# Turned blocks of experts, x and y in pieces of 512 bytes: contraction tiles that hold every fourth unit

## The reference

```
x = x + (x @ W[cat] + b[cat])                       # layer 0: W[cat] is 512 x 512
h = gelu(x @ fc1_w.T + fc1_b)                       # 512 -> 2048, exact gelu
x = x + concat(h @ fc2_w.T + fc2_b,                 # 2048 -> 384, shared
               h @ experts_w[e].T + experts_b[e])   # 2048 -> 128, the batch's expert (128 x 2048)
```

## Time and profile before

| | |
|---|---|
| median of three runs | 1680.95 us |
| profiled execution | 1681.4 us |
| its span, first to last instruction | 1679.6 us |
| granted TensorE clock, mean | 0.997 |
| DMA packets, bytes | 884,826, 243.44 MB |

### The profile page before, as it was taken

One profiled execution on the slowest core, in us unless ns is written; L12 is line 12 of the kernel. 1 busy time (PEld: TensorE's weight loads), 2 busy tenths in 40 slices (PEclk: granted clock), 3 DMA queues, 4 the chain that ended last, 5 costly groups with the idle time before them and its releaser, 6 DMA issues.

```text
span 1679.6 us, 28015 instructions
## 1 busy us (share of the span) xinstructions
PE 1639.4 (98%) x7065; PEld 1315.8 (78%) x7065; DVE 1176.4 (70%) x2004; ACT 551.9 (33%) x927; POOL 195.1 (12%) x195
## 2 busy tenths in 40 slices
PE   7899999999999999999999999999999999999999
PEld 5778887877878778787877878778787787878887
DVE  5677667776777767776776677767777677767754
ACT  4343333333323333333332333333333333333321
POOL 0200100111020010200102001110200102001110
PEclk9999999999999999999999999999999999999999
DMA  7886776757677575775767767686775757757630
GB/s 207 185 190 150 147 149 147 156 129 162 127 163 151 131 156 118 167 159 133 149 133 160 156 144 157 131 157 135 163 153 131 155 118 164 163 131 151 134 61 26
DMA packets 884826, 243.44 MB, mean 145 GB/s; under 512 B 803688, under 2 KB 818168, under 8 KB 884732
## 3 DMA queue, kind: packets, MB, share of 16 engines
q1 hardware_dynamic: 740732, 203.75, 57.1%
q10 hardware_dynamic: 144000, 38.82, 10.7%
HBM read 209.93 MB, written 32.51 MB: 144 GB/s over the span
## 4 chain that ended last, share of the span: by engine, by line
PE 66%; SPq 20%; issue 8%; DMA 3%; DVE 2%; ACT 1%; DVEq 0%
PE ps_out L814 30%; PE ps_h L799 14%; PE ps_e L799 13%; PE ps_y L786 8%; SPq L386 8%; SPq L341 4%; SPq L320 2%; DMA e_blocks<-in_L_cond_experts_w 2%; SPq L399 2%; SPq L351 1%; SPq L393 1%; PE ps_t L745 1%; DVE e_whole L643 1%; DVE h L599 1%; DVE w2e L599 1%
## 5 line engine op out<-in xcount | busy, mean ns | idle before, releaser
L814 PE MATMUL ps_out<-w2e,h 128*128 128x512 f32 x3072 | 758.0, 396 | 10.0 <-DVE h L599 10.0
L814 PEld LDWEIGHTS ps_out<-w2e,h 128*128 128x128 f32 x3072 | 574.3, 188 | 152.5 <-DVE h L599 15.9
L799 PE MATMUL ps_e<-y_t,w 128*128 128x512 f32 x1536 | 376.8, 395 | 1.4 <-DVE y_t L599 1.4
L799 PE MATMUL ps_h<-y_t,w 128*128 128x512 f32 x1536 | 375.7, 394 | 0.0
L799 PEld LDWEIGHTS ps_e<-y_t,w 128*128 128x128 f32 x1536 | 290.7, 189 | 66.9 <-DVE y_t L599 1.6
L799 PEld LDWEIGHTS ps_h<-y_t,w 128*128 128x128 f32 x1536 | 288.5, 188 | 65.7
L643 DVE STREAM_TRANSPOSE e_whole<-e_blocks 128x512 f32<-128x512 f32 x256 | 182.0, 711 | 109.3 <-DMA e_blocks<-in_L_cond_experts_w 100.9
L530 ACT CAST w2e<-e_whole 128x512 fp32r<-128x512 f32 x256 | 158.6, 620 | 284.4 <-PE ps_out L814 157.4
L463 POOL TENSOR_TENSOR x_raw<-x_raw,b_all 128x512 f32<-128x512 f32 x60 | 85.3, 1422 | 1354.9 <-DMA x_raw<-in_x 1303.2
L499 ACT CAST w_split<-w_raw 128x512 fp32r<-128x512 f32 x244 | 145.7, 619 | 243.7 <-DMA w_raw<-in_L_cond_W 174.4
L599 DVE TENSOR_TENSOR w_split<-w_raw,w_split 128x512 fp32r<-128x512 f32 x244 | 161.1, 688 | 84.6 <-ACT w_split L499 83.7
(11 more groups left out here) (71 smaller groups left out, 431.3 us busy)
## 6 DMA issues: line engine op xcount, KB each, us to landing
e_blocks<-in_L_cond_experts_w SPq DMA_DIRECT2D x1024, 64.0 KB, 2.9
w_raw<-in_L_cond_W SPq DMA_DIRECT2D x248, 256.0 KB, 2.9
out<-resid SPq DMA_DIRECT2D x64, 256.0 KB, 4.7
x_blocks<-in_x SPq DMA_DIRECT2D x240, 64.0 KB, 2.4
b_all<-in_L_cond_b SPq DMA_DIRECT2D x60, 256.0 KB, 4.3
x_raw<-in_x SPq DMA_DIRECT2D x60, 256.0 KB, 4.6
y_rows<-y ACTq DMA_DIRECT2D x60, 256.0 KB, 2.8
x_blocks<-y_rows ACTq DMA_DIRECT2D x240, 64.0 KB, 3.7
```

The source lines that it names most:

```text
L799: last = nc.tensor.matmul(h_bank(c)[:, :], w1[:, w, k, c * P:(c + 1) * P], y_t[:, a, k, :, :].rearrange("p b s -> p (b s)"), start=(k == 0 ...
L814: last = nc.tensor.matmul(ps_out[b][:, :], h[:, c % 2, a, b * S:(b + 1) * S], fc2_columns(c, c % 2, w, b), start=(c == 0 and n == 0), stop ...
```

## The change

Contraction tile k now holds the units 4p + k, for partition p. The same holds for the hidden units: tile c of quad u holds the units 512u + 4p + c % 4. The sum over units is the same, in another order. A quad of an expert is then 512 hidden units in a row, and a block's piece in the loads is 128 elements, 512 bytes, of which DVE's transpose takes every fourth. TensorE's transposes read every fourth column of the tile. Rows of layer 0's weights and of fc1_w come four apart, fc2_w in rows of 2 KB; fc1_b goes directly to b1, in pieces of four values.

```diff
-        b1_rows = x_raw[0:NC, 0:P]
...
-        def hidden_rows(c):
-
-            return (c % QUAD) * (NC // QUAD) + c // QUAD
+        def every_fourth(whole, k):
+
+            return whole.rearrange("p (m k) -> p k m", k=KD)[:, k]
 
         def prep_src(t):
             if PREP[t][0] == "fc1":
-                m = hidden_rows(PREP[t][1])
-                return fc1_w[m * P:(m + 1) * P, :]
+                m = PREP[t][1]
+                return fc1_w.rearrange("(u p c) d -> u c p d", u=NC // QUAD, c=QUAD)[m // QUAD, m % QUAD]
             _, n, q = PREP[t]
-            return fc2_w[n * P:(n + 1) * P, :].rearrange("p (k u h) -> u p k h", k=QUAD, h=P)[q]
+            return fc2_w[n * P:(n + 1) * P, q * QUAD * P:(q + 1) * QUAD * P]
...
-                    src = x[bass.ds(G * GB + b, 1), :, :].rearrange("o (j q) (k i r) -> i q k (o j) r", q=Q, k=KD, r=Q)[i]
-                    sp.dma_start(x_blocks[i * Q:(i + 1) * Q, :].rearrange("q (k j r) -> q k j r", k=KD, r=Q), src)\
+                    src = x[bass.ds(G * GB + b, 1), :, :].rearrange("o (j q) (i n) -> i q (o j) n", q=Q, n=P)[i]
+                    sp.dma_start(x_blocks[i * Q:(i + 1) * Q, :].rearrange("q (j n) -> q j n", n=P), src)\
...
-                sp.dma_start(w_slot(G, j), l0_w[bass.ds(cat, 1), k * P:(k + 1) * P, :].rearrange("o d n -> (o d) n"))\
+                src = l0_w[bass.ds(cat, 1), :, :].rearrange("o (p k) n -> k (o p) n", k=KD)[k]
+                sp.dma_start(w_slot(G, j), src)\
...
-                            .rearrange("o (j q) (c u i r) -> u i q c (o j) r", q=Q, c=QUAD, i=P // Q, r=Q)[quad, i]
-                        sp.dma_start(e_blocks[i * Q:(i + 1) * Q, quad % 2, b, :]
-                                     .rearrange("q (c j r) -> q c j r", c=QUAD, r=Q), src).then_inc(e_in[quad % 2], 16)
+                            .rearrange("o (j q) (u i n) -> u i q (o j) n", q=Q, i=P // Q, n=P)[quad, i]
+                        sp.dma_start(e_blocks[i * Q:(i + 1) * Q, quad % 2, b, :].rearrange("q (j n) -> q j n", n=P), src)\
+                          .then_inc(e_in[quad % 2], 16)
...
-                    sp.dma_start(b1_rows, fc1_b.rearrange("(c p) -> c p", p=P)).then_inc(b1_in, 16)
+                    sp.dma_start(b1[:, :].rearrange("p (u c) -> p u c", c=QUAD), fc1_b.rearrange("(u p c) -> p u c", p=P, c=QUAD))\
+                      .then_inc(b1_in, 16)
...
-                    src = y_rows[b, :, :].rearrange("(j q) (k i r) -> i q k j r", q=Q, k=KD, r=Q)[i]
-                    act.dma_start(x_blocks[i * Q:(i + 1) * Q, :].rearrange("q (k j r) -> q k j r", k=KD, r=Q), src)\
+                    src = y_rows[b, :, :].rearrange("(j q) (i n) -> i q j n", q=Q, n=P)[i]
+                    act.dma_start(x_blocks[i * Q:(i + 1) * Q, :].rearrange("q (j n) -> q j n", n=P), src)\
...
-                if j == 2:
-                    act.wait_ge(b1_turned, 1)
-                    nc.scalar.copy(b1[:, :], ps_e[:, 0:NC]).then_inc(b1_ready, 1)
             y_high(0, GB - 1)
-            act.wait_ge(b1_ready, 1)
+            act.wait_ge(b1_in, 16)
...
+            def split_of(whole_t):
+
+                return whole_t.rearrange("p (k j q) -> p k j q", k=KD, q=Q)
+
+            def blocks_of(blocks):
+
+                return blocks.rearrange("p (j r k) -> p k j r", k=KD, r=Q)
...
-                nc.vector.transpose(x_whole_t[:, :], x_blocks[:, :]).then_inc(x_turned, 1)
+                nc.vector.transpose(split_of(x_whole_t[:, :]), blocks_of(x_blocks[:, :])).then_inc(x_turned, 1)
...
-                nc.vector.transpose(dst, x_blocks[:, :]).then_inc(y_turned, 1)
+                nc.vector.transpose(split_of(dst), blocks_of(x_blocks[:, :])).then_inc(y_turned, 1)
...
-                off = (c % QUAD) * P
-                nc.vector.transpose(e_whole[:, :], e_blocks[:, (c // QUAD) % 2, :, off:off + P]).then_inc(e_turned, 1)
+                src = e_blocks[:, (c // QUAD) % 2, :, :].rearrange("p b (j r c) -> p c (b j) r", c=QUAD, r=Q)[:, c % QUAD]
+                nc.vector.transpose(e_whole[:, :].rearrange("p (a q) -> p a q", q=Q), src).then_inc(e_turned, 1)
...
-                turn(ps_t, [resid[:, b, k * P:(k + 1) * P] for k in range(KD)]).then_inc(x_turned, 1)
+                turn(ps_t, [every_fourth(resid[:, b, :], k) for k in range(KD)]).then_inc(x_turned, 1)
...
-                turn(y_bank(b), [y[:, b, k * P:(k + 1) * P] for k in range(KD)])\
+                turn(y_bank(b), [every_fourth(y[:, b, :], k) for k in range(KD)])\
...
-                turn(prep_bank(t), [prep_tile(t)[:, n * P:(n + 1) * P] for n in range(4)]).then_inc(prep_turned, 1)
+                turn(prep_bank(t), [every_fourth(prep_tile(t), k) for k in range(KD)]).then_inc(prep_turned, 1)
...
-                if j == 2:
-                    pe.wait_ge(b1_in, 16)
-                    nc.tensor.transpose(ps_e[:, 0:NC], b1_rows, ident[0:NC, 0:NC]).then_inc(b1_turned, 1)
```

More of the change, by code:

```diff
@@ L312, in load_prep @@
             after(eng, prep_turned, max(prep_earlier(t), default=-1) + 1)
[L313 to L314 removed]
+            eng.dma_start(prep_tile(t), prep_src(t)).then_inc(prep_in[prep_slot(t)], 16)
         @block.sync
```

8 lines of the change are left out of this document (1 added, 7 removed).

## The result

The changed kernel takes 1670.62 us (median of five runs, 1668.82 to 1672.98), the kernel before 1681.01 beside it: ratio 0.9937, 95% interval 0.9922 to 0.9952. That is 10.4 us faster, where 24 were forecast. The profiled execution took 1670.62 us, its span 1668.8.

A forecast was written before the change was run, and what follows sets the result against it. TensorE, 98% busy, was taken as the bound, losing time to waits behind DVE. 17.5 us in the loop's groups + 5.5 + 1.4 in group 0 = 24.4 us off 1681.4: 1657.0 us, range 1647 to 1679.

The forecast's parts named there:

- group 0: First group: a 3.40 us wait and 2.1 us of low clock go (5.5 us), plus a 1.4 us prepared-tile wait.
- the first stall: Step 3 of a group: fc2 waits for h_low behind DVE's late expert blocks; 0.65 us a group, to go.
- The floor: TensorE's time for a group without waits: 36 calls of 2.80 us, 100.8 us against 102.07, so 1.27 us lost.
- The second stall: Start of a group: TensorE waits for x_low behind layer 0's late-issued slices; 0.62 us a group, to go.
- the cover: SP's issue ahead of layer 0's slices: 24 DMAs save 0.25 us each, 6.0 us where 0.9 is needed.
- nothing added: DVE's transposes at a step of four stay at 711 ns; the other end was 0.53 us more each.
- covered: Weight rows 8 KB apart land nothing to 1 us later, hidden by SP coming 5 to 6 us earlier.
- 2d - 0.45: Stall in us at a group's start if each DVE transpose takes d longer; 1.7 where 0.62 stood for the third cycle.
- the other end: Upper bound for TensorE's own strided transposes: twice as long, 36 x 0.43 = 15.5 us; the forecast added nothing.
- The second cycle: Rival, chance 0.31: DVE's strided transposes take 0.53 us more each, only the first stall goes; 1669.6 us.
- The third cycle: Rival, chance 0.11: DVE's strided transposes take 1.07 us more each, the kernel gets slower; 1699 us.
- the unchanged issue time: Rival, chance 0.12: a block DMA holds SP as long as before, the stalls mostly stay; 1675 us.

The follow-up runs named there:

- experiment 3: The changed kernel with DVE's transposes reading runs and layer 0's slices loaded as 128 consecutive rows (units mixed, wrong result): 1656.43 us, ratio 0.9837.
- experiment 18: The changed kernel with layer 0 as before the change, and the experts' bias loads and batch 0's x load issued later: 1657.32 us, ratio 0.9857.
- experiment 1: The changed kernel with only DVE's transposes of experts, x and y reading runs again (units mixed, wrong result): 1664.34 us, ratio 0.9883.
- experiment 2: The changed kernel with only layer 0's slices loaded as 128 consecutive rows again (units mixed, wrong result): 1666.75 us, ratio 0.9903.
- experiment 17: The changed kernel with the experts' bias loads and batch 0's x load issued later: 1664.34 us, ratio 0.9898.
- experiment 15: The changed kernel with the experts' bias loads moved behind the next group's first slices and stores: 1666.80 us, ratio 0.9909.
- experiment 16: The changed kernel with layer 0 as before the change and the experts' bias loads moved behind the next group's first slices and stores: 1670.70 us, ratio 0.9930.
- experiment 5: The kernel before the change, unaltered, profiled once more to see what differs between executions: 1684.21 us.
- experiment 13: The changed kernel with each expert block DMA in 256 evenly spaced pieces of 256 bytes, pattern kept at three dimensions (wrong result): 1688.77 us, ratio 1.0035.
- experiment 14: The changed kernel with each experts' bias load cut into two loads of 128 pieces of 256 bytes: 1704.67 us, against 1687.61 for the kernel before.
- experiment 10: A change of the same kind with tiles of every second unit, pieces of 256 bytes and slice rows 4 KB apart: 1677.35 us, ratio 0.9954.

## Why the prediction was wrong

The forecast counts 17.5 us in the groups of the loop and 6.9 in group 0. Measured in the profiles, from the first call of layer 0 in one group to that of the group thirteen later, 11.1 us are won (167.27 to 1493.72 us before, 168.62 to 1483.99 after), 1.1 behind it, and 1.4 are lost ahead of it.

*What bounds the kernel, and the first stall: right.* TensorE's waits behind DVE were the loss, 19.6 us by their rows. The wait for h_low went whole, 10.0 us where 9.1 were counted, and with it DVE's wait for blocks. Block DMAs take SP 317 ns for 333 forecast, packets are 303,178 for 307,000, the DMA share from 128 to 1600 us fell from 0.69 to 0.52, for 0.47 forecast. The chain's call of fc2 doesn't come every 100.8 us yet: TensorE's calls behind x_low's wait stand at 269.80 and, eleven groups later, at 1383.27: (1383.27 - 269.80) / 11 = 101.2.

*The floor: 0.7 us a group too high.* "36 x 2.80 = 100.8" takes the longest calls for all. Without a wait a group takes 100.11 us in experiment 3 and 100.19 in experiment 18: calls of fc1 take 2.74 to 2.80 us, and one of layer 0 takes 1.38. So the kernel before lost 102.03 - 100.11 = 1.92 us a group, not 1.27, and the waits were worth more than was counted. This is why experiment 3 meets the forecast's 1657.0: it wins 25.0 us in thirteen groups, where 1.27 x 13 = 16.5 were counted, and nothing in group 0, where 6.9 were. The two errors cancel; the agreement is luck.

*The second stall: wrong.* 0.62 x 14 = 8.7 us were to go, and nothing did: 9.6 us before, 9.6 after. Three steps failed. The first is the cover, "24 DMAs (20 of experts, 4 of x) x 0.25 = 6.0 us" ahead of the slices. The saving per DMA was right, but SP comes 2.1 us earlier, not 6.0: 16 of the 24 stand ahead of a wait for the buffer, and what they save turns into that wait (32.8 us to 115.9 us in all); the eight behind it save 8 x 0.265 = 2.1. I had counted issue time and not asked what SP would meet when faster. The second is "nothing added" for DVE's transposes. They cost 0.385 us each, between the two ends; two of them lie between h_low and x_low. The third is "covered": the slices' rows 8 KB apart land 1.1 us later (2.9 to 4.0 us), within my bound, but under the true cover of 2.1 us that, with the transposes, is enough to keep the stall. Experiments 1 to 3 separate the two: of the 9.6 us behind x_low the slices alone keep 3.3, the transposes alone 4.3 (1.3 of it POOL's), and with both undone 0.6 are left. The prediction's formula for the stall, 2d - 0.45, gives 0.32 us for the measured d = 0.385; experiments 2 and 17 list waits of 0.20 to 0.24, and the next call comes 0.36 to 0.40 late.

A fourth part was in no step: POOL's sums beside DVE's, 0.8 to 1.1 us on an x_low each time. In the changed kernel one falls on x_low twice, once with a wait (1279.30). They are a part of why moving the bias alone gave less than expected in experiment 15, and are why it cost time in 16. Over the whole run a low half of a slice takes 856 ns where it took 688, most of it where TensorE doesn't wait.

*Group 0: wrong, 6.9 us counted, none won.* The wait of 3.40 us and the lower clock went (the window 70 to 75 us is at 1.00), but the chain now has 2.46 us at 82.90, and the wait of 1.4 us for a prepared tile stays:

```profile
73.14 0.47 PE ps_t L748 x4
...
82.90 2.46 issue
```

TensorE's first call of layer 0 behind a wait for x_low in the loop stands at 269.35 before and at 269.80 after: in the first 270 us nothing was won. This execution starts fc1 3.4 us later, which experiment 5 leaves open as the change's or not; counted from there, 2.0 us were won by the loop's first group (167.27 and 168.62 us), and the rest went into waits such as those above. I had taken one execution's waits there as the change's to remove. TensorE's transposes went from 0.43 to 0.47 us a four, 1.4 us for 36: not nothing, but far from the other end.

*The rivals.* The second cycle's mechanism came nearest: the first stall goes, the second stays, 1669.6 for 1670.62 measured, though the transposes took 1096 ns and not 1240. That its number is met is partly luck: it had the transposes alone keep the stall, where late slices make 6.7 of the 9.6 us, and it counted 2.7 us of gain in group 0, where there was none. The third cycle and the unchanged issue time are excluded by the rows. That the access pattern costs and not its pieces is excluded by experiments 13 and 14.

*b1* holds SP 402 ns at 5.0 us, and nothing is seen to wait for it.

## What to carry to other kernels

Issue time saved on a queue is worth only what lies behind the queue's last wait for a buffer: look for the next wait in that queue before multiplying. Costs that are to hide in slack are added up along their chain, and the slack is measured after the change's own timing: here it was 2.1 us, not 6. A floor is read from a stretch without waits, not from the longest call times their number, and a forecast's number that is met is checked term by term before it is believed. Where two engines slow each other, an earlier transfer can make a kernel slower (experiment 16). A layout that helps the loads of one stage need not be used in all: here experts and y gain by it, and layer 0, whose slices it spreads, does better without.

## What the runs showed of the hardware

DVE's 32 x 32 transpose of 512 fp32 elements a partition takes 711 ns at a step of one or two elements, 1.08 to 1.10 us at four, 1.2 us at eight. A DMA of 64 KB holds SP's queue 317 to 333 ns with 128 pieces and 564 to 582 with 256 or 512 (on ACT's 453 and 658 ns with 128 and 512). TensorE's load of a 128 x 128 fp32 tile takes 209 ns (median) at a step of four columns, 140 without, four transposes in a row 0.47 us for 0.43. A DMA of 256 KB with rows of 2 KB lands in 2.8 to 2.9 us (median) when they are in a row, 3.3 when they are 4 KB apart (experiment 10), 3.9 to 4.0 at 8 KB.

DVE's sum of two operands in SBUF that begins while a sum on POOL runs ends 0.54 to 0.56 us behind POOL's end, as if it had waited for it; alone it takes 0.68. In experiment 18 POOL's ends at 1277.83 + 1.56 = 1279.39, and h_low, begun at 1278.28, ends at 1279.95. Where DVE's begins first it is POOL's that is longer: at 471.56 us in the changed kernel 1.74 us, beside an x_low of 0.68 begun at 471.48, and at most groups' starts of the kernel before 1.29 to 1.31. The Trainium skill, *SBUF — State Buffer*, section "SBUF: two separate sides", has this as an exclusive lock on a shared pair of ports, taken by whichever starts first, a DVE operation with two SBUF inputs or one of GpSimd that reads SBUF, while the other blocks whole; the rows agree, but that 0.56 us are 0.12 less than a whole sum.
